# Turning the layers' input whole, and one block of programs with the weights converted between the first batch's steps

## The chip, the cores and the metric

The kernel runs on one core of one Trainium2 chip. The metric is device time of one execution in microseconds (us). A core has five engines with programs of their own: TensorE (PE, matmuls and transposes into the eight PSUM banks), VectorE (DVE), ScalarE (ACT), GpSimd (POOL), and SyncE (SP), which here only issues DMAs. They meet by semaphores: an instruction raises one when it is done, and another engine waits for a value of it. Each engine runs its instructions strictly in the order in which they are written, so a wait holds everything behind it.

## The reference

Sixteen batches of 512 rows by 128 columns. Linear attention with 16 heads of 8, then two layers of windowed softmax attention (8 heads of 64, window 64) and a gated feed-forward. All of it is between layer norms, with residual sums.

```python
def shift_token(t):                      # the upper half of the columns comes from the row before
    t1, t2 = jnp.split(t, 2, axis=-1)
    t2 = jnp.pad(t2, ((0, 0), (1, 0), (0, 0)))[:, :-1]
    return jnp.concatenate([t1, t2], axis=-1)

def _layer(x, wqkv, qs, ksc, wo, lg, lb, w1, b1, w2, b2):
    h = shift_token(x)
    q, k, v = jnp.split(h @ wqkv, 3, axis=-1)
    ...                                  # heads, l2norm, rotary_xpos, local_attention
    x = x + o @ wo
    h = shift_token(x)
    h = (h - mu) / jnp.sqrt(var + 1e-05) * lg + lb
    a, g = jnp.split(h @ w1 + b1, 2, axis=-1)
    return x + (a * jax.nn.gelu(g, approximate=False)) @ w2 + b2

x = x + _layernorm(_L0_attn_ref(_layernorm(x), Wq, Wk, Wv, Wo))
y = _layernorm(x)
for l in range(2): y = _layer(y, ...)
out = x + _layernorm(y)
```

## The kernel before

**Steps.** The work on a batch is cut into steps, each known by kind, layer l, part j (a quarter of the 512 rows) and batch n. Linear attention: load (x_in), ln_in and norm_in (to y_rows), yt (turned to y_cols), aqkv, arope, phi, at, aq, den, expand, as (scores), mask, ao, awo, then ln_attn, norm_attn, add_mid, keep (a copy of x_in goes to DRAM), ln_mid and norm_mid (to x_res0, the layers' input). Per layer: h (the input turned, shifted by a row in the upper half, and split), per quarter qkv, sq, ss, guess, norms, rope, normalize, qkt (q and k turned), s (scores), max, exps, rden, pn, pt (probabilities turned), o, wo; then sh, ln_ffn, norm_ffn, h2t, w1, gelu, gate, w2. At the end ln_out, norm_out, bring, add_out, store.

**Order.** STARTS gives each batch a start and TIMES gives each step of each engine a time in a batch. `order_of` sorts all steps of an engine by their sum; that is the engine's program, written out in full. Some four batches are in work at once. HOLD says how long a step is meant to hold its PSUM bank; `banks_of` gives out the eight banks by it, and `take` makes PE wait for the step that used the bank before (RELEASED names the signal).

**Signals.** `Signal` makes one semaphore per layer. They start at a value of four batches (`start`), so that waits on earlier steps of the first batches hold at once; 128 semaphores are raised so.

**The turn h.** On PE (lines 709 to 722) the bank's lower 64 partitions get four transposes of columns 0 to 63 (line 721). Its upper 64 get matmuls of columns 64 to 127 with the identity, one row further on (line 719), so that the shift lies in where the result is put; a one-column matmul of an identity with a column whose upper half is zero clears row 0 (line 716). ACT copies the bank to h_cols as float16 (line 911), DVE takes the rest that this leaves, bank minus copy, as a second float16 (line 1134). qkv (line 732) multiplies in three passes per 512 columns: high by high, high by low weights, then low by high weights, the first to wait for DVE.

**Linear weights and layer weights.** They live in SBUF once: w_la and wo_la_t are turned on PE, wqkv and w1 are scaled and split into two float16 halves by ACT (line 533) and DVE (line 545), the rotary tables are multiplied by the q and k scales (line 557), the masks and an identity are cast (lines 547 to 549). The kernel has two blocks. The first one loads all weights with one semaphore (38 DMAs), converts them, clears buffers and starts the signals; the second runs the steps. Between blocks all engines meet.

## Time and profile before

| | us |
|---|---|
| median of 3 runs | 1832.37 (1830.87 to 1837.60) |
| the profiled execution, its own time | 1839.22 |
| its span, first to last instruction | 1836.7 |
| granted PE clock, mean over the span | 0.971 |
| x_in loads issued at | 35.68, 87.52, 172.70, 273.74, 377.93, 481.87, ... 1523.3 |

The page gives busy time per engine, a chain of work that ended last, and groups of instructions. A timeline gives each engine's instructions in order of time, equal neighbours merged (x8 means eight of them); behind a row in brackets stands how long the engine had been idle and what released it. The loads of x_in mark the batches: their distance is the time of one batch.

### The profile page before, as it was taken

How to read it: one execution, taken by the hardware profiler on the slowest of the kernel's cores; microseconds unless marked ns; L12 is line 12 of the kernel's file. 1: busy time of each engine (PE TensorE's matmuls, PEld its weight loads, DVE VectorE, ACT ScalarE, POOL GpSimd, SP SyncE). 2: the span in 40 equal slices, each digit the busy share in tenths (PEclk: the TensorE clock that was granted, in tenths of full speed). 3: DMA queues.
4: the chain of work that ended last, by engine and by line, in shares of the span. 5: the costliest groups of instructions: out<-in, count | busy, mean ns of one | idle time of the engine just before them, and what ended most of it. 6: DMA issues, size and time to landing. Idle time of an engine off the chain costs nothing.

```text
span 1836.7 us, 51372 instructions
## 1 busy us (share of the span) xinstructions
PE 1641.0 (89%) x18212; PEld 1149.2 (63%) x18340; DVE 1329.3 (72%) x3471; ACT 1367.3 (74%) x4277; POOL 1285.8 (70%) x1715
## 2 busy tenths in 40 slices
PE   0677989999999999999999999999999999998875
PEld 0344666666667666666666666666667666666653
DVE  2465777877777787877778787777777787776552
ACT  1264768787887878798887878787787878788663
POOL 1263777777777887777777787777777887777562
PEclk9888999999999999999999999999999999999986
DMA  3000001011111011111111011111101011111001
GB/s 117 12 16 19 22 23 25 18 36 30 36 28 28 19 34 27 31 36 30 36 28 28 19 31 30 31 36 28 39 22 31 22 25 36 30 31 30 19 21 29
DMA packets 58135, 54.52 MB, mean 30 GB/s; under 512 B 7538, under 2 KB 42780, under 8 KB 57756
## 3 DMA queue, kind: packets, MB, share of 16 engines
q1 hardware_dynamic: 57884, 51.25, 11.0%
q8 instruction: 149, 2.44, 0.5%
q14 instruction: 102, 0.84, 0.2%
HBM read 13.48 MB, written 8.39 MB: 12 GB/s over the span
## 4 chain that ended last, share of the span: by engine, by line
PE 70%; ACT 12%; POOL 7%; issue 6%; DVE 3%; DMA 0%; POOLq 0%; ACTq 0%; DVEq 0%; SPq 0%
PE bank L732 10%; PE bank L787 7%; PE bank L759 7%; PE bank L798 5%; PE bank L744 5%; PE bank L771 5%; PE bank L838 4%; PE bank L827 4%; PE bank L679 4%; PE bank L695 3%; PE bank L753 2%; PE bank L719 2%; ACT probs L959 2%; ACT probs_t L853 2%; POOL qk_rows L1308 2%
## 5 line engine op out<-in xcount | busy, mean ns | idle before, releaser
L959 ACT ACTIVATE probs<-bank,s_low 128x128 f32<-128x128 f32 x1024 | 360.1, 384 | 60.7 <-DVE s_low L1171 60.6
L1308 POOL TENSOR_TENSOR qk_rows<-qk_rows,qk_tmp 128x512 f32<-128x512 f32 x256 | 328.2, 1282 | 16.6 <-DVE qk_tmp L1159 15.8
L1321 POOL TENSOR_TENSOR probs<-probs,s_rden 128x512 f32<-128x512 f32 x256 | 263.5, 1050 | 68.1 <-DVE s_rden L1180 68.1
L732 PE MATMUL bank<-wqkv_sb,h_cols 128*128 128x512 f16 x1152 | 281.2, 388 | 7.9 <-ACT probs_t L853 2.6
L1311 POOL TENSOR_TENSOR qk_rows<-qk_rows,qk_rnorm 128x512 f32<-128x512 f32 x256 | 268.7, 1050 | 20.1
L959 ACT ACTIVATION_READ_ACCUMULATOR probs<-bank,s_low 128x1 f32 x1024 | 229.0, 224 | 0.0
L1156 DVE TENSOR_TENSOR qk_rows<-bank,rope 128x512 f32<-128x512 f32 x256 | 174.4, 681 | 39.2 <-POOL qk_rows L1311 35.4
L1126 DVE TENSOR_TENSOR room<-bank,const 128x512 f32<-128x512 f32 x256 | 158.7, 683 | 57.8 <-PE bank L679 56.2
L732 PEld LDWEIGHTS bank<-wqkv_sb,h_cols 128*128 128x128 f16 x1152 | 108.2, 99 | 142.7 <-issue 22.7
L853 ACT ACTIVATE probs_t<-bank 128x512 f32<-128x512 f32 x256 | 140.9, 598 | 67.9 <-PE bank L771 65.2
L1142 DVE TENSOR_REDUCE qk_sum<-qk_sq 128x16 f32<-128x1024 f32 x128 | 155.1, 1212 | 46.2 <-ACT qk_sq L918 44.2
L1171 DVE TENSOR_REDUCE s_low<-bank 128x4 f32<-128x512 f32 x256 | 164.3, 684 | 30.6 <-PE bank L759 30.6
L1159 DVE TENSOR_TENSOR qk_tmp<-bank,rope 128x512 f32<-128x512 f32 x256 | 174.3, 681 | 0.0
L918 ACT ACTIVATE qk_sq<-bank 128x512 f32<-128x512 f32 x256 | 144.4, 618 | 22.9 <-PE bank L732 22.2
L798 PE MATMUL bank<-wo_sb,o_cols 128*128 128x128 f32 x1024 | 141.0, 281 | 19.4 <-DVE room L1126 12.5
L744 PE MATMUL bank<-const,qk_rows 128*128 128x128 f32 x1024 | 140.8, 281 | 15.4 <-POOL qk_rows L1311 12.6
L798 PEld LDWEIGHTS bank<-wo_sb,o_cols 128*128 128x128 f32 x1024 | 129.5, 195 | 38.1 <-DVE room L1126 24.9
L771 PE MATMUL bank<-const,probs 128*128 128x128 f32 x1024 | 142.5, 280 | 8.8 <-POOL probs L1321 6.8
L787 PE MATMUL bank<-probs_t,v_even 128*64 128x64 f32 x2048 | 133.2, 228 | 17.6 <-ACT probs_t L853 10.1
L759 PEld LDWEIGHTS bank<-k_cols,q_cols 64*64 64x64 f32 x4096 | 112.3, 134 | 55.5 <-issue 55.5
L759 PE MATMUL bank<-k_cols,q_cols 64*64 64x128 f32 x4096 | 143.4, 278 | 0.0
L827 PE MATMUL bank<-h_cols,w_sb 128*128 128x512 f16 (+1 forms) x576 | 139.6, 386 | 2.1 <-ACT h_cols L990 0.9
(154 smaller groups left out, 3650.6 us busy)
## 6 DMA issues: line engine op xcount, KB each, us to landing
v_even<-v_rows SPq DMA_DIRECT2D x224, 128.0 KB, 2.3
x_in<-in_L_attn_x SPq DMA_DIRECT2D x16, 256.0 KB, 3.2
kept_rows<-x_in SPq DMA_DIRECT2D x16, 256.0 KB, 2.3
x_back<-kept_rows SPq DMA_DIRECT2D x16, 256.0 KB, 3.0
out<-x_back SPq DMA_DIRECT2D x16, 256.0 KB, 2.4
room<-in_constants SPq DMA_DIRECT2D x1, 1024.0 KB
hidden<-in_L_ffn_wqkv SPq DMA_DIRECT2D x1, 768.0 KB
qk_rows<-in_L_ffn_wqkv SPq DMA_DIRECT2D x1, 768.0 KB
```

Source lines behind the costliest of these rows:

```text
L732: mm = pe.matmul(to[:, :], h_cols[st.l][:, x_half, st.j * P:(st.j + 1) * P], wqkv_sb[:, st.l, w_half, w * INNER:(w + 1) * INNER], start=(n ...
L744: mm = pe.transpose(to[:, c * P:(c + 1) * P], qk_rows[st.l][:, a, w, c * P:(c + 1) * P], ident)
L759: mm = pe.matmul(to[half][w * WIN:(w + 1) * WIN, c * P:(c + 1) * P], q_cols[st.l][rows, a, c, w * WIN:(w + 1) * WIN], k_cols[st.l][rows, c ...
L771: mm = pe.transpose(to[:, c * P:(c + 1) * P], probs[st.l][:, half * PAIRS + c, :], ident)
L787: mm = pe.matmul(to[half * DH:(half + 1) * DH, c * P + w * WIN:c * P + (w + 1) * WIN], values[l][:, a, head * DH:(head + 1) * DH], probs_t ...
L798: mm = pe.matmul(to[:, 0:D], o_cols[st.l][:, c * P:(c + 1) * P], wo_sb[:, st.l, c, :], start=(c == 0), stop=(c == PAIRS - 1))
L827: mm = pe.matmul(to[0:n, :], w1_sb[:, st.l, w_half, half * HID + at_:half * HID + at_ + n], h2_cols[:, x_half, :], start=(p == 0), stop=(p ...
L853: return act.activation(to, of, ACT.Copy)
L959: act.activation(probs[st.l][:, n, :], bank[b[half]][:, c * P:(c + 1) * P], ACT.Exp, bias=s_low[st.l][:, a, n:n + 1], accum_out=s_sum[st.l ...
L1308: pool.tensor_tensor(rows(w), rows(w), qk_tmp[l][:, w, :], ALU.add).then_inc(pool_qk.of(st), 1)
L1311: pool.tensor_tensor(heads64(rows(w)), heads64(rows(w)), qk_rnorm[l][:, a, w * HEADS:(w + 1) * HEADS].unsqueeze(2).to_broadcast([P, HEADS, ...
L1321: pool.tensor_tensor(probs[l][:, mine, :], probs[l][:, mine, :], s_rden[l][:, a, mine].unsqueeze(2).to_broadcast([P, PAIRS, P]), ALU.mult) ...
```

## The change

**The turn.** PE does four whole transposes of 128 by 128 into the bank; the matmuls of lines 716 and 719 go. The shift moves to ACT and DVE: each does its work in two instructions, one for the lower 64 partitions and 512 columns, one for the upper 64 partitions, which reads bank columns 0 to 510 and writes h_cols columns 1 to 511. Column 0 of the upper half is cleared once at the start. act_h and dve_h count two per batch, and qkv waits for both.

**One block.** The first block is gone. SP loads the first batch's x_in, the four linear weights and the constants, then the weights of layer 0, then of layer 1, each group with a semaphore of its own. Each engine starts its own signals. The weights wait in buffers of layer 1 (qk_rows1, probs1, probs_t1, qk_tmp1, o_cols1) that no batch needs yet, where before they lay in `room`. ACT splits layer 0's weights after the fourth av and layer 1's after the first ao of batch 0; DVE does its part after den 1, mask 0, mask 3 and ln_mid of batch 0. The first qkv and rope of each layer wait for it.

**The table.** STARTS, TIMES and HOLD are all new.

```diff
-STARTS = [8839, 22968, 37104, 51237, ...
+STARTS = [3891, 18013, 32146, 46280, ...
...
-        "h": [[17736], [35934]],
+        "h": [[16859], [35929]],
...
-        act_h = signal("act_h", DEPTH, 1)
+        act_h = signal("act_h", DEPTH, 1, 2)
...
-        dve_h = signal("dve_h", DEPTH, 1)
+        dve_h = signal("dve_h", DEPTH, 1, 2)
...
-        setup_const = room[:, 4 * D:4 * D + NSETUP]
+        setup_const = qk_rows[1][:, :, :, :].rearrange("p a w n -> p (a w n)")[:, 0:NSETUP]
+        la_rows = o_cols[1]
...
-        with nc.Block() as block:
-            @block.sync
-            def _(sp):
-                sp.dma_start(const[:, :], consts[:, 0:NCONST]).then_inc(loaded, 16)
...
+        def start_signals(engine, mine):
+            for sig in every:
+                if sig.name.split("_")[0] in mine:
                     for sem in sig.sems:
+                        engine.sem_inc(sem, sig.start())
...
+                start_signals(sp, ("x", "out", "v", "sh"))
+                for at, (_, st) in enumerate(order["sync"]):
+                    if at > 0:
+                        run(st)
+                        continue
+                    sp.dma_start(x_in[:, :, :], rows_of(x, st)).then_inc(x_loaded.of(st), 16)
+                    load_first()
+                    for l in range(DEPTH):
+                        load_layer(l)
+                    sp.wait_ge(zeroed, ZEROED)
...
-                    pe.matmul(to[DH:P, 0:1], ident[:, DH:P], cst("causal")[:, 0:1], start=True, stop=True)
                     for j in range(NT):
-                        n = min(P, T - 1 - j * P)
-                        pe.matmul(to[DH:P, j * P + 1:j * P + 1 + n], x_res[st.l][0:n, j, DH:D], ident[0:n, 0:n],
-                                  start=True, stop=True)
-                        mm = pe.transpose(to[0:DH, j * P:(j + 1) * P], x_res[st.l][:, j, 0:DH], ident)
+                        mm = pe.transpose(to[:, j * P:(j + 1) * P], x_res[st.l][:, j, :], ident)
                     mm.then_inc(pe_h.of(st), 1)
...
+                start_signals(pe, ("pe",))
+                pe.wait_ge(first_loaded, 16 * FIRST_LOADS)
+                for n in range(4):
+                    mm = pe.transpose(bank[0][:, n * D:(n + 1) * D], la_rows[:, n * D:(n + 1) * D], ident)
+                mm.then_inc(turned, 1)
+                pe.wait_ge(la_ready, 2)
                 for _, st in order["tensor"]:
+                    if st.kind == "qkv" and st.n == 0 and st.j == 0:
+                        pe.wait_ge(ready[st.l], READY[st.l])
...
-                    copy(h_cols[st.l][:, 0, :], bank[b[0]][:, :]).then_inc(act_h.of(st), 1)
+                    copy(to[0:DH, 0, :], bank[b[0]][0:DH, :]).then_inc(act_h.of(st), 1)
+                    copy(to[DH:P, 0, 1:T], bank[b[0]][DH:P, 0:T - 1]).then_inc(act_h.of(st), 1)
...
+                def halve(l):
+                    act.wait_ge(loaded[l], 16 * LOADS[l])
+                    for whole, halves in ((whole_wqkv[l], wqkv_sb[:, l, :, :]), (whole_w1[l], w1_sb[:, l, :, :])):
+                        act.activation(halves[:, 0, :], whole, ACT.Copy, scale=W_SCALE).then_inc(halved, 1)
...
+                    if st.name() == ("av", 0, NT - 1, 0):
+                        halve(0)
+                    if st.name() == ("ao", 0, 0, 0):
+                        halve(1)
...
-                    dve.tensor_tensor(h_cols[st.l][:, 1, :], bank[b[0]][:, :], h_cols[st.l][:, 0, :],
+                    dve.tensor_tensor(to[0:DH, 1, :], bank[b[0]][0:DH, :], to[0:DH, 0, :],
+                                      ALU.subtract).then_inc(dve_h.of(st), 1)
+                    dve.tensor_tensor(to[DH:P, 1, 1:T], bank[b[0]][DH:P, 0:T - 1], to[DH:P, 0, 1:T],
                                       ALU.subtract).then_inc(dve_h.of(st), 1)
...
+                dve.wait_ge(first_loaded, 16 * FIRST_LOADS)
+                dve.wait_ge(zeroed, ZEROED)
+                turn_linear()
                 for _, st in order["vector"]:
+                    if st.kind == "rope" and st.n == 0 and st.j == 0:
+                        dve.wait_ge(ready[st.l], READY[st.l])
                     run(st)
+                    if st.name() == ("den", 0, 1, 0):
+                        lower_weights(0)
+                    if st.name() == ("mask", 0, 0, 0):
+                        turn_tables(0)
+                        turn_masks()
+                    if st.name() == ("mask", 0, 3, 0):
+                        lower_weights(1)
+                    if st.name() == ("ln_mid", 0, 0, 0):
+                        turn_tables(1)
```

On PE, layer 0's turn in the middle of the run, before (line 798 is wo, 732 is qkv):

```order
L716 MATMUL bank1<-const 64x1 [waits act_ln_mid_0,dve_wo_1]
L719 MATMUL bank1<-const,x_res0 64x128
L721 MATMUL bank1<-const,x_res0 64x128
...
L721 MATMUL bank1<-const,x_res0 64x128
L798 MATMUL bank5<-wo_sb,o_cols1 128x128 [waits act_o_1,act_p_1]
L798 MATMUL bank5<-wo_sb,o_cols1 128x128 x3
L732 MATMUL bank3<-wqkv_sb,h_cols0 128x512 [waits act_p_1,act_h_0]
L732 MATMUL bank3<-wqkv_sb,h_cols0 128x512
L732 MATMUL bank3<-wqkv_sb,h_cols0 128x512 [waits dve_h_0]
```

and after (line 678 is the turn, 755 is wo, 689 is qkv):

```order
L678 MATMUL bank4<-const,x_res0 128x128 [waits act_ln_mid_0,act_p_1]
L678 MATMUL bank4<-const,x_res0 128x128 x3
L755 MATMUL bank0<-wo_sb,o_cols1 128x128 [waits act_o_1,dve_wo_1]
L755 MATMUL bank0<-wo_sb,o_cols1 128x128 x3
L689 MATMUL bank2<-wqkv_sb,h_cols0 128x512 [waits act_o_1,act_h_0]
L689 MATMUL bank2<-wqkv_sb,h_cols0 128x512
L689 MATMUL bank2<-wqkv_sb,h_cols0 128x512 [waits dve_h_0]
```

The turn is four instructions for nine matmul and transpose calls; behind it stand the same wo and qkv, with the same wait for dve_h at the third pass.

On ACT, from norm_mid (x_res0) to the next batch's norm_in (y_rows), before:

```order
L864 ACTIVATE x_res0<-x_in,ln_nmr_mid0,ln_rstd_mid0 128x128 [waits pool_rstd_mid_0,dve_wo_0]
L864 ACTIVATE x_res0<-x_in,ln_nmr_mid0,ln_rstd_mid0 128x128 x3
L959 ACTIVATE probs1,s_sum1<-bank7,s_low1 128x128 [waits dve_max_1,pe_pt_1]
...
L959 ACTIVATE probs1,s_sum1<-bank0,s_low1 128x128 [waits dve_max_1]
...
L853 ACTIVATE o_cols1<-bank1 128x512 [waits pe_wo_1,pe_o_1]
L853 ACTIVATE h_cols0<-bank6 128x512 [waits pe_h_0]
L938 ACTIVATE v_rows1<-bank3 128x512 [waits v_low1_1,pe_o_1,pe_qkv_1]
L990 ACTIVATE h2_cols<-bank4,ln_cols 128x512 [waits pe_w1_1,pe_h2t_0]
L990 ACTIVATE h2_rows<-bank4,ln_cols 128x512
L864 ACTIVATE y_rows<-x_in,ln_nmr_in0,ln_rstd_in0 128x128 [waits pool_rstd_in_0,pool_xmid_0]
```

and after:

```order
L829 ACTIVATE x_res0<-x_in,ln_nmr_mid0,ln_rstd_mid0 128x128 [waits pool_rstd_mid_0,dve_wo_0]
L829 ACTIVATE x_res0<-x_in,ln_nmr_mid0,ln_rstd_mid0 128x128 x3
L926 ACTIVATE probs1,s_sum1<-bank0,s_low1 128x128 [waits dve_max_1,pe_pt_1]
...
L926 ACTIVATE probs1,s_sum1<-bank6,s_low1 128x128 [waits dve_max_1]
...
L818 ACTIVATE o_cols1<-bank2 128x512 [waits pe_wo_1,pe_o_1]
L818 ACTIVATE h_cols0<-bank0 64x512 [waits pe_h_0]
L818 ACTIVATE h_cols0<-bank0 64x511
L957 ACTIVATE h2_cols<-bank5,ln_cols 128x512 [waits pe_w1_1,pe_h2t_0]
L957 ACTIVATE h2_rows<-bank5,ln_cols 128x512
L829 ACTIVATE y_rows<-x_in,ln_nmr_in0,ln_rstd_in0 128x128 [waits pool_rstd_in_0,pool_xmid_0]
...
L905 ACTIVATE v_rows1<-bank4 128x512 [waits v_low1_1,pe_o_1,pe_qkv_1]
```

h is two copies, and the copy of v (v_rows1) has moved behind y_rows.

On DVE, in the first batch behind den 1 (line 1119 before, 1097 after), before:

```order
L1119 RECIPROCAL la_rden<-la_rden 128x16 [waits dve_aden_0]
L1126 TENSOR_TENSOR room<-bank,const 128x512 [waits pe_as_0,pe_ao_0]
L1126 TENSOR_TENSOR room<-bank,const 128x512 [waits pe_as_0] x3
L1126 TENSOR_TENSOR room<-bank,const 128x512 [waits pe_as_0,pe_ao_0]
L1126 TENSOR_TENSOR room<-bank,const 128x512 [waits pe_as_0] x3
```

and after:

```order
L1097 RECIPROCAL la_rden<-la_rden 128x16 [waits dve_aden_0]
L1226 TENSOR_SCALAR b_cols<-b_cols 128x1 [waits weights_loaded_0]
...
L1230 SCALAR_TENSOR_TENSOR wqkv_sb<-hidden,wqkv_sb 128x1536 [waits weights_halved]
L1230 SCALAR_TENSOR_TENSOR w_sb<-probs,w_sb 128x682 [waits weights_halved]
L1076 SCALAR_TENSOR_TENSOR la_phi<-la_tb,la_phi 128x256 [waits act_aexp_0]
L1104 TENSOR_TENSOR room<-bank,const 128x512 [waits pe_as_0,pe_ao_0]
L1104 TENSOR_TENSOR room<-bank,const 128x512 [waits pe_as_0] x3
L1239 SCALAR_TENSOR_TENSOR rope<-qk_rows,qk_tmp 128x64 x16
L1245 CAST ident_h<-const 128x128
L1246 CAST mask_h<-qk_rows 128x512
...
L1104 TENSOR_TENSOR room<-bank,const 128x512 [waits pe_as_0,pe_ao_0]
L1104 TENSOR_TENSOR room<-bank,const 128x512 [waits pe_as_0] x3
```

The splitting of layer 0's weights (line 1230) stands ahead of the third phi and of the first mask, the tables and casts (1239 to 1247) between the first two masks.

## Rows read from the trace of the kernel before

**Rows 1.** The page, part 1: busy us, share of the span, instructions.

```profile
PE 1641.0 (89%) x18212; PEld 1149.2 (63%) x18340; DVE 1329.3 (72%) x3471; ACT 1367.3 (74%) x4277; POOL 1285.8 (70%) x1715
```

**Rows 2.** Busy time by stretches: start:end, length, engines busy (instructions), PEclk, DMA share, GB/s.

```profile
4.00:6.00 2.00, 0.00 (x0) 0.00 (x0) 0.00 (x0) 0.00 (x0) 2.00 (x2) 1.00 0.96 368
...
36.00:89.00 53.00, 27.97 (x233) 16.99 (x233) 24.08 (x84) 12.28 (x34) 13.33 (x18) 0.87 0.04 12
482.00:585.90 103.90, 99.66 (x1140) 70.59 (x1147) 82.56 (x214) 84.73 (x268) 79.98 (x106) 1.00 0.12 30
```

**Rows 3.** Waits of PE, 482 to 586 us: total, times, longest (us).

```profile
PE bank L640 <- ACT y_rows L864: 1.0, 1, 1.0
...
PE bank L787 <- ACT probs_t L853: 0.3, 1, 0.3
```

**Rows 4.** Timeline of PE around layer 0's turn: start, length (us), engine, line, operation.

```profile
466.73 1.16 PE L705 MATMUL bank<-wo_la_t,y_cols 128*128 128x128 f32 x8
...
484.00 0.28 PE L716 MATMUL bank<-const 128*64 128x1 f32 x2
...
486.40 1.06 PE L798 MATMUL bank<-wo_sb,o_cols 128*128 128x128 f32 x8
487.29 2.37 PE L732 MATMUL bank<-wqkv_sb,h_cols 128*128 128x512 f16 x9
490.69 0.63 PE L640 MATMUL bank<-const,y_rows 128*128 128x128 f32 x4 [1.02 <-ACT y_rows L864]
491.15 1.04 PE L771 MATMUL bank<-const,probs 128*128 128x128 f32 x8
```

**Rows 5.** Timeline of ACT, DVE and POOL beside it.

```profile
480.15 1.65 ACT L864 ACTIVATE x_res<-x_in,ln_nmr_mid,ln_rstd_mid 128x128 f32<-128x128 f32 x4
...
484.44 0.61 ACT L853 ACTIVATE o_cols<-bank 128x512 f32<-128x512 f32 x1
...
485.01 0.87 DVE L1027 BATCH_NORM_STATS2 ln_stats_in<-x_in 128x6 f32<-128x128 f32 x4 [2.08 <-DMA x_in<-in_L_attn_x]
...
486.48 0.19 DVE L1180 RECIPROCAL s_rden<-s_sum 128x8 f32<-128x8 f32 x1
...
486.60 0.60 ACT L853 ACTIVATE h_cols<-bank 128x512 f16<-128x512 f32 x1 [1.54 <-PE bank L721]
...
487.23 0.69 DVE L1134 TENSOR_TENSOR h_cols<-bank,h_cols 128x512 f16<-128x512 f32 x1 [0.56 <-ACT h_cols L853]
...
487.73 0.20 POOL L1250 TENSOR_TENSOR ln_nmr_in<-ln_nmr_in,ln_rstd_in 128x4 f32<-128x4 f32 x1
...
488.90 1.65 ACT L864 ACTIVATE y_rows<-x_in,ln_nmr_in,ln_rstd_in 128x128 f32<-128x128 f32 x4
```

**Rows 6.** Groups of one batch, 482 to 586 us, shapes apart: busy us, mean ns.

```profile
L1000 ACT ACTIVATE hidden<-bank,b_cols 128x512 f32<-128x512 f32 x4 | 2.5, 684 | 0.0
...
L1000 ACT ACTIVATE hidden<-bank,b_cols 85x512 f32<-85x512 f32 x2 | 1.4, 685 | 0.1
```

**Rows 7.** Timeline of the start: loads and the first statistics.

```profile
0.72 0.40 SPq L484 DMA_DIRECT2D const<-in_constants  x1
...
19.70 0.43 SPq L502 DMA_DIRECT2D room<-in_L_ffn_k_scale  x1
...
35.68 0.38 SPq L588 DMA_DIRECT2D x_in<-in_L_attn_x  x1
38.50 0.87 DVE L1027 BATCH_NORM_STATS2 ln_stats_in<-x_in 128x6 f32<-128x128 f32 x4 [3.13 <-DMA x_in<-in_L_attn_x]
```

**Rows 8.** Timeline of the start: conversions, and the first batch's masks.

```profile
22.90 1.49 ACT L533 ACTIVATE wqkv_sb<-hidden 128x1536 f16<-128x1536 f32 x1 [20.91 <-DMA room<-in_L_ffn_k_scale]
...
24.42 1.76 DVE L545 SCALAR_TENSOR_TENSOR wqkv_sb<-hidden,wqkv_sb 128x1536 f16<-128x1536 f32 x1 [1.25 <-ACT wqkv_sb L533]
...
30.31 4.39 DVE L557 SCALAR_TENSOR_TENSOR rope<-room 128x64 f32<-128x64 f32 x32
...
57.74 4.88 DVE L1126 TENSOR_TENSOR room<-bank,const 128x512 f32<-128x512 f32 x8 [2.12 <-PE bank L679]
```

More of the change, by code:

```diff
@@ L163 @@
[L163 to L170 removed]
+        "norm_in": [[3712]],
@@ L474, in build @@
[L474 removed]
+        whole_w1 = [of[:, :, :].rearrange("p h n -> p (h n)")[:, 0:2 * HID] for of in (probs[1], probs_t[1])]
+        qk_scale = qk_tmp[1][:, :, :].rearrange("p w n -> p (w n)")[:, 0:DEPTH * 2 * DH].rearrange(
             "p (l w c) -> p l w c", l=DEPTH, w=2)
[L476 removed]
+        first_loaded = ctx.enter_context(nc.semaphore("first_loaded"))
```

322 lines of the change are left out of this document (161 added, 161 removed), and 32 rows, old and new, of tables (HOLD, TIMES).

## The prediction

> **What bounds the kernel now.** Read the busy shares of the page first [rows 1]: TensorE (PE) is busy 89% of the span, the three others 70 to 74%. Then the busy time by stretches [rows 2]. The span has three parts. Up to 36 us the weights are loaded and converted and no batch runs. From 36 to 89 us the first batch goes alone through linear attention and PE works 28 of 53 us: latency sets the pace. In the middle a batch takes 104.0 us (x_in is loaded every 104 us), and of 103.9 us PE is busy 99.7; ScalarE (ACT) 84.7, VectorE (DVE) 82.6. So in the middle an instruction less on PE is worth its time, as long as PE doesn't then wait. PE waits little there; its longest named wait is 1.0 us, for y_rows of the next batch [rows 3].
>
> The profiled execution took 1839.2 us, of which 1836.7 are span; I sum against 1839.2. The median of the runs shown is 6.9 us below it, and I take 6.9 off at the end.
>
> **The layer's turn on PE.** Before, a turn (h) begins at 484.00 and the next step at 486.40: 2.40 us of PE [rows 4]. Its replacement is four whole transposes, the same four instructions as the turn of y_rows, which begins at 490.69 and gives way at 491.15: 0.46 us. That is 1.94 us less PE, twice per batch, 32 times in all.
>
> **What ACT and DVE pay.** Each copy of the turned bank becomes two, over 64 partitions and 512 or 511 columns. A copy's time doesn't go by partitions: the same gelu took 684 ns on 128 partitions and 685 on 85 [rows 6]. So each half costs a whole one: ACT +0.5 to 0.6 us per turn, DVE +0.6 to 0.7 (their rows are 0.60 and 0.69, and neighbours overlap by some 0.1) [rows 5]. Per batch ACT goes to 85.9 and DVE to 84.0 us: neither becomes the bound by its load. What counts is who waits for the two copies.
>
> **Layer 0: the gain is lost to a path.** On PE the turn is followed by one step (wo, 0.89 us) and then by the qkv matmuls, whose third pass waits for the lower half from DVE; that is so before and after. Follow the path from the end of norm_mid (x_res, 481.80) [rows 5]: it frees x_in, the next batch's rows are loaded, DVE takes its statistics at 485.01 (+3.2), is free behind a reciprocal at 486.6 (+4.8), and only then comes DVE's part of h, 487.23 to 487.92 (+6.1). PE's first qkv group runs from 487.29 and, with 2.37 us where the others take 2.10, waits 0.25 in it. After, DVE is free at +4.8 and does two halves, 1.3 us: +6.1 again. So the third pass can't come earlier than +6.2, whatever PE saves before. Nor does the part ahead shrink: from the end of awo (467.89) to the end of norm_mid are 13.9 us of DVE, POOL and ACT in a row, in the same order before and after, with the same PE steps beside them. ACT makes PE wait already at wo: it has exps (2.75 us) and the copy of o between norm_mid and the h copies, o_cols is there at +3.3, wo can begin at +3.4 instead of +2.6, qkv at +4.5. I book 0 for layer 0's turn; its bounds are -1.94 (no wait) and +0.7 (DVE is late by a whole half).
>
> One wait goes: PE's y step came at 490.69, +8.9, held by ACT, which did h, v, two h2 copies and then y_rows at 488.90. In the new order v stands behind y_rows, so y_rows can begin when POOL has the scale (487.73 + 0.20, or +6.1) and ACT is free: h at +3.3 to +4.4, h2 to +5.7, then y_rows +6.2 to +7.8. qkv's last pass leaves PE about then. PE's y step at +7.95: 0.95 us sooner. Bounds 0 and -1.0 [rows 3].
>
> **Layer 1: the gain stays.** There several steps stand between the turn and qkv, in both orders (some 12 us of PE work), so nobody waits for the longer copies: -1.94.
>
> Per batch in the middle: -1.94 - 0.95 = -2.9, a period of 101.1. Bounds -3.9 (all PE time of both turns) and 0 (the new order waits as much more elsewhere; see the rivals). Sixteen batches, less one for the ends, where PE isn't the bound: 15 x 2.9 = -43.5 (0 to -58).
>
> **The order's table.** All steps are placed anew and so are the banks, but on PE the sequence of kinds is nearly the one before. Where a step now stands closer behind what it needs (s one step behind the last qkt of a layer-1 round, o one step behind a layer-0 pt), the trace of before shows what such a distance costs: o one step behind its pt waited 0.3 us [rows 3]; other pairs moved apart. I book 0, within -15 and +30 over the run, worth -1 to +2 us a batch.
>
> **The start.** Before, DVE's first statistics are at 38.50: all loads are in by 22.9, then the weights are converted, then x_in is issued at 35.68 [rows 7, 8]. After, x_in is SP's first load, then four small weights and the constants, 866 KB in all; issues follow each other by 0.5 us (38 issues from 0.72 to 19.70), the queues move 368 GB/s [rows 2], so 2.4 us of transfer, and a load of x_in lands 2.8 us after its issue (35.68 to 38.50). SP first raises 18 of the 128 signals; all 128 took less than the 15.6 us from 20.13 to 35.68 [rows 7], so 18 take under 2.2. Landed at 6.5 to 10; PE's four transposes (0.46 at full clock, twice that at half) and two DVE copies of 384 and 128 columns (0.8, by the 0.69 of 512) make 1.3 to 2: statistics at 8.5 to 12, and at up to 13 if loads behind slow it. I take 9.5: -29.0 (-25.5 to -30).
>
> The conversions (ACT 4.5 us, DVE some 11) go between the first batch's steps [rows 8]. In the first batch's own time, as before: ACT's first pair (1.49 for 1536 columns, 0.7 for 682) delays la_phi and la_qk_cols by 1.0. DVE's first pair (1.76 for 1536 columns, 0.8 for 682) now stands ahead of the third la_phi and of mask: mask can start at 58.7 instead of 57.74, +1.0, the same delay. Half the tables (2.2 of 4.39) and three casts (0.9), 3.1 us, stand between the first two masks, which ran back to back for 4.88 us: all of it on the path. Later edits hide: DVE's second pair in the 3.1 us before ln_attn's statistics, the second half of the tables behind ln_mid while POOL and ACT work; a further 0.6 for what doesn't. Sum +4.7 (bounds +2 if the masks aren't on the path, +9 if loads come late). Loads: ACT needs layer 0's weights at about 22 us; everything was landed at 22.9 before, and layer 0's half is now issued first.
>
> Sum: 1839.2 - 29.0 + 4.7 - 43.5 = 1771.4; less 6.9: **1765**.
>
> **A rule against the change.** In the middle of the run the granted clock is 1.00 (2.4 GHz); in the first batch, where PE pauses, it is 0.87 on average [rows 2]. If the new turns ran at 1.2 GHz, each would cost 0.92 us instead of 0.46: 0.9 us per batch. The Trainium skill (TensorE: Matmul & The Clock Gate, "Part 4: PE-mode transpose") says that transposes don't count as PE being busy for the clock. By that rule, more transposes and fewer matmuls speak for a lower clock; the 1.00 of the middle stretch, where each batch turns q, k and the probabilities by transposes, speaks against it.
>
> **Rivals.**
> - B, the period stays at 104: waits grow by 2.9 us a batch in the new order. For it: PE had 4 us of slack a batch, the others wait for each other on paths like layer 0's, which already eats one turn. Then only the start gains: 1839.2 - 24.3 - 6.9 = 1808.
> - C, everything is had: 3.9 us a batch: 1765 - 15 = 1750. For it: the new order was free to put work between turn and qkv elsewhere. Against: the third pass.
> - D, slower: at layer 0 PE has only its o step and the short turn (1.5 us) while ACT does norm_mid, exps and the copy of o (1.65 + 2.75 + 0.6 = 5.0 us) before wo may start. Before, the wo of the round ahead, s and the long turn stood there too, 6 us with the o step (480.4 to 486.40). If PE comes to o just when ACT has turned the probabilities, it waits 3.5 us there, and if the same happens at s behind qkt and at the layer-1 rounds, 6 us a batch are lost: 1808 + 15 x 3.1 = 1854. It decides from 4.5 us of new waits a batch on (2.9 + 24.3 / 15).
> - E, the clock: the turns run at 1.2 GHz: 1765 + 15 x 0.9 = 1779.
> - F, the loads of the layers or the conversions hold the first batch up, +9 to +14: 1770 to 1780.
>
> **Chances.** Forecast 0.55, B 0.2, C 0.1, D 0.05, E 0.03, F 0.07. The range reaches from below C to just past B, 1745 to 1812, and leaves out D and tails. About 0.5% (9 us) is what a measurement of this kernel can tell from no change: faster than 1823 0.92, within 0.04, slower 0.04.
>
> **What would show it.** ln_stats_in first at 8.5 to 12 us; x_res of batch 0 ends near 63 (87.4 before, less 24.3); x_in loads 101 us apart; the turn 0.46 us on PE; in the first qkv group of a batch PE waits for h_cols of ACT and DVE, some 2 us in all, at layer 1 not at all; the wait for y_rows gone; clock 1.00. Wrong if the period is 103 or more, if it is near 100 with no wait at h, or if the first batch's end moved by under 18 us.

## The result, and the profile after

| | before | after |
|---|---|---|
| median of 14 runs each | 1835.1 us (1830.9 to 1837.7) | 1847.3 us (1839.0 to 1852.3) |
| ratio | 1 | 1.0063 [1.0049, 1.0078] |
| the profiled execution, its span | 1836.7 | 1839.2 |
| granted PE clock, mean | 0.971 | 0.951 |
| first statistics at | 38.50 | 10.06 |
| second load of x_in (norm_mid of batch 0 over) | 87.52 | 70.04 |
| distance of the loads in the middle | 104.0 | 105.8 |

The change made the kernel 0.6% slower; the forecast was 1765 (1745 to 1812). The profile of after gained 17.5 us by the second load and gave 21.0 back between it and the last one (1526.8, before 1523.3). It is one of the faster executions of after (1841.0 us, at a granted clock of 0.951; the median of the fourteen is 1847.3 at 0.946), so its trace shows 6 us less of the loss than the medians do.

The page of after, PE's busy time and its clock in 40 slices (9 is 90% or more):

```profile
PE 1653.1 (90%) x18020; PEld 1161.9 (63%) x18020; DVE 1373.9 (75%) x3503; ACT 1383.7 (75%) x4309; POOL 1281.4 (70%) x1717
...
PEclk8798999999999999999999999999999999999988
```

PE is busy for longer than before (1641.0 us) although it has less to do [rows 1], and the clock's digits show 9 for the whole middle, as before. The finer view shows what happens. These are the stretches of one batch, from one load of x_in to the next (columns as in [rows 2], PEclk third from the end):

```profile
468.52:472.90 4.38, 2.32 (x42) 1.84 (x41) 1.83 (x12) 4.33 (x20) 0.00 (x0) 1.00 0.28 90
472.90:476.30 3.40, 3.03 (x11) 2.26 (x12) 2.59 (x8) 3.18 (x7) 3.12 (x4) 0.53 0.00 0
476.30:517.40 41.10, 39.97 (x394) 27.45 (x392) 35.05 (x85) 36.38 (x119) 32.48 (x47) 1.00 0.13 31
517.40:520.80 3.40, 3.40 (x40) 2.61 (x37) 2.57 (x4) 1.71 (x8) 3.32 (x4) 0.51 0.00 0
```

Twice in a batch, for 3.4 us, PE runs at a granted clock near 0.5, which is 1.2 GHz; before, this stretch had 1.00 [rows 2]. The first time lies 4 to 8 us behind the load, the second 49 to 52. Not every batch looks like this one: of ten, six have both stretches, one has the second alone, and in three (from 786.0, 892.2 and 997.9) the first is 6.8 us long and the second is missing. PE's named waits in the batch shown:

```profile
PE bank L755 <- DVE x_att L1166: 2.4, 1, 2.4
PE bank L640 <- DVE room L1104: 0.5, 1, 0.5
```

The wait for y_rows [rows 3] is gone, as forecast; a wait of 2.4 us for x_att at wo, line 755, has come in its place. PE around layer 0's turn (compare [rows 4]):

```profile
470.19 0.66 PE L678 MATMUL bank<-const,x_res 128*128 128x128 f32 x4
473.27 2.08 PE L755 MATMUL bank<-wo_sb,o_cols 128*128 128x128 f32 x8 [2.43 <-DVE x_att L1166]
475.14 2.80 PE L689 MATMUL bank<-wqkv_sb,h_cols 128*128 128x512 f16 x9
477.77 0.60 PE L601 MATMUL bank<-const,y_rows 128*128 128x128 f32 x4
```

The turn (470.19) ends after 0.66 us and then PE stands still for 2.4. The step it waits with is wo of layer 1, round 1 (wo11). Its bank was last used by wo10, the wo of the round ahead, and DVE gives that back late:

```profile
471.47 0.87 DVE L1005 BATCH_NORM_STATS2 ln_stats_in<-x_in 128x6 f32<-128x128 f32 x4 [2.47 <-DMA x_in<-in_L_attn_x]
...
472.94 0.28 DVE L1166 TENSOR_TENSOR x_att<-x_res,bank 128x128 f32<-128x128 f32 x1
...
473.25 0.63 DVE L1113 TENSOR_TENSOR h_cols<-bank,h_cols 64x512 f16<-64x512 f32 x1
473.91 0.69 DVE L1115 TENSOR_TENSOR h_cols<-bank,h_cols 64x511 f16<-64x511 f32 x1
```

In the new order DVE adds wo10 (x_att, 472.94) behind the statistics of the next batch, which wait for the load that norm_mid frees; before, it stood ahead of them (482.64, statistics at 485.01 [rows 5]):

```profile
482.64 0.29 DVE L1185 TENSOR_TENSOR x_att<-x_res,bank 128x128 f32<-128x128 f32 x1 [1.72 <-PE bank L798]
```

The other place is the first linear-attention score step, as of round 0 (as00). It has four row groups, and the table gives each of them a bank:

```profile
510.15 0.66 PE L678 MATMUL bank<-const,x_res 128*128 128x128 f32 x4
510.64 0.59 PE L710 MATMUL bank<-mask_h,ident_h 128*128 128x512 bf16 x2
...
514.78 1.52 PE L640 MATMUL bank<-room,la_qk_cols 32*128 32x512 f32 x4
516.75 1.39 PE L640 MATMUL bank<-room,la_qk_cols 32*128 32x512 f32 x4 [0.45 <-DVE room L1104]
```

The third group takes the bank of the first and waits for DVE to mask it. With the old order the four have four banks and run beside each other in 1.14 us (here in e4, which keeps the old order):

```profile
508.03 1.14 PE L640 MATMUL bank<-room,la_qk_cols 32*128 32x512 f32 x8 [0.26 <-DVE h_cols L1115]
```

The start (compare [rows 7] and [rows 8]), first statistics and first mask:

```profile
10.06 0.86 DVE L1005 BATCH_NORM_STATS2 ln_stats_in<-x_in 128x6 f32<-128x128 f32 x4
```

```profile
36.87 2.48 DVE L1104 TENSOR_TENSOR room<-bank,const 128x512 f32<-128x512 f32 x4 [2.90 <-PE bank L640]
```

### The profile page after: what moved, and what is told of

The parts are those of the page before. It is cut to its first block, busy times and chain, and to the rows that moved or that the text cites. A ratio compares the mean times of both kernels' runs of the same rounds, so it can differ in the third digit from the quotient of the medians.

```text
span 1839.2 us, 50920 instructions
## 1 busy us (share of the span) xinstructions
PE 1653.1 (90%) x18020; PEld 1161.9 (63%) x18020; DVE 1373.9 (75%) x3503; ACT 1383.7 (75%) x4309; POOL 1281.4 (70%) x1717
## 3 DMA queue, kind: packets, MB, share of 16 engines
q1 hardware_dynamic: 57884, 51.25, 10.8%
## 4 chain that ended last, share of the span: by engine, by line
PE 64%; ACT 15%; POOL 7%; issue 6%; DVE 5%; DMA 3%; SPq 0%; POOLq 0%; ACTq 0%; DVEq 0%
PE bank L689 12%; PE bank L640 5%; PE bank L716 5%; PE bank L744 5%; PE bank L701 5%; PE bank L755 5%; ACT probs L926 5%; PE bank L795 5%; PE bank L728 4%; PE bank L784 4%; PE bank L656 3%; DMA x_in<-in_L_attn_x 3%; PE bank L710 2%; POOL probs L1349 2%; ACT probs_t L818 2%
## 5 line engine op out<-in xcount | busy, mean ns | idle before, releaser
L689 PE MATMUL bank<-wqkv_sb,h_cols 128*128 128x512 f16 x1152 | 289.7, 399 | 10.2 <-DVE h_cols L1115 5.8
L755 PE MATMUL bank<-wo_sb,o_cols 128*128 128x128 f32 x1024 | 152.0, 295 | 45.9 <-DVE x_att L1166 34.6
L755 PEld LDWEIGHTS bank<-wo_sb,o_cols 128*128 128x128 f32 x1024 | 137.3, 206 | 60.6 <-DVE x_att L1166 37.7
L744 PE MATMUL bank<-probs_t,v_even 128*64 128x64 f32 x2048 | 139.7, 235 | 10.2 <-ACT probs_t L818 5.1
L701 PE MATMUL bank<-const,qk_rows 128*128 128x128 f32 x1024 | 136.0, 278 | 9.4 <-POOL qk_rows L1339 9.1
L744 PEld LDWEIGHTS bank<-probs_t,v_even 128*64 128x64 f32 x2048 | 110.7, 144 | 48.7 <-issue 17.8
```

The source lines that it names most:

```text
L689: mm = pe.matmul(to[:, :], h_cols[st.l][:, x_half, st.j * P:(st.j + 1) * P], wqkv_sb[:, st.l, w_half, w * INNER:(w + 1) * INNER], start=(n ...
L701: mm = pe.transpose(to[:, c * P:(c + 1) * P], qk_rows[st.l][:, a, w, c * P:(c + 1) * P], ident)
L744: mm = pe.matmul(to[half * DH:(half + 1) * DH, c * P + w * WIN:c * P + (w + 1) * WIN], values[l][:, a, head * DH:(head + 1) * DH], probs_t ...
L755: mm = pe.matmul(to[:, 0:D], o_cols[st.l][:, c * P:(c + 1) * P], wo_sb[:, st.l, c, :], start=(c == 0), stop=(c == PAIRS - 1))
```

## The experiments

"Old order" is the table of times and banks of before, "new order" that of after. Every kernel was timed beside before on the same chip; before's own median on these chips lay between 1834.9 and 1836.8 us, so medians of different rows compare to some 2 us. "Undisturbed" periods are the distances of x_in loads in the middle of the profiled execution in which the clock stayed at 1.00; the last two columns count, of ten or eleven such distances, those with PE near half clock at the first place (from 4 to 7 us behind the load on) and at the second (from 48 to 51 on).

| kernel | median, us | ratio to before | undisturbed period | 1st | 2nd |
|---|---|---|---|---|---|
| before | 1835 | 1 | 103.9 to 104.4 | 0 | 0 |
| e1 turn alone | 1819.1 | 0.991 [0.990, 0.993] | 102.3 to 103.4 | 1 | 0 |
| e2 new order alone | 1859.2 | 1.014 [1.011, 1.017] | 104.6 to 105.0 | 1 | 2 |
| e3 start alone | 1818.2 | 0.991 [0.989, 0.993] | 103.6 to 104.9 | 0 | 0 |
| e4 start and turn, old order | 1798.2 | 0.980 [0.978, 0.983] | 102.3 to 103.4 | 0 | 0 |
| e5 start and new order, old turn | 1841.2 | 1.003 [1.002, 1.004] | 105.0, 105.2 | 6 | 2 |
| after | 1847.3 | 1.006 [1.005, 1.008] | none | 9 | 7 |

**The three parts, one at a time.** e1 takes before and changes the turn only, e2 the two tables only, e3 the start only, e4 is after with the old tables, e5 after with the old turn.

> The kernel before with only the turn changed: four whole transposes on PE, each copy on ACT and DVE in two halves; old order and banks, old start. Theory O (the new order and banks cost the time, the turn helps): period 101 to 102 us instead of 104, total 1835 less 30 to 45 = 1790 to 1805, granted clock of the middle 1.00. Theory T (the turn itself costs: later copies, or a lower clock because PE pauses behind a shorter turn): period 105 to 106, total 1850 to 1865, granted clock about 0.97 as in the changed kernel.

> The kernel before with only the table of the order and the banks of after; old turn, old start. Theory O: the table costs about 5 us a batch more than the turn gives back: period 107 to 109, total 1880 to 1915, PE waits of 2 us or more at wo for DVE's x_att in each batch and two stretches at half clock. Theory T: period 103 to 104, total 1820 to 1835, clock 1.00.

> The kernel before with only the start changed: x_in loaded first, one block, conversions between the steps of the first batch; old order, banks and turn. Both theories: the middle stays at 104 us a batch and 1.00 of clock, and the total falls by what the start gains: 28.4 at the first statistics less what the conversions cost the first batch. If that is the 4.7 of the forecast, 1835 - 24 = 1811; if it is the 10.9 that the changed kernel shows and the order has no part in it, 1835 - 17.5 = 1817.

> The changed kernel with the order and banks of before: new start, new turn. Theory O: both gains, period 101 to 102, total 1770 to 1790, well below both kernels. Theory T: only the start is had and the turn costs 1.9 us a batch: 1817 + 30 = 1847, as the changed kernel.

> The changed kernel with the old turn (nine matmuls and transposes, one copy each on ACT and DVE): new start, new order and banks. If the new order costs the same beside either turn, the period is the 105.0 of the table alone, the granted clock of the middle 1.00, and the total 1859 less 17 = 1842. If the two stretches at half clock come from the order and not from the turn, the clock is 0.97 here too and the total 1855 or more.

The start is worth 17 us, the turn 16, both together 37 (e4, 2% below before and the fastest design found); the 4 us by which the two together exceed their sum are not explained. The turn gives some 1.4 us a batch in either order where the clock is undisturbed (104.0 to 102.7; in the new order 105.0 to the 103.5 of e6 and e11 below). The new order costs 24 us alone and 49 beside the new start and turn. So theory O holds in its sign but not in its numbers: e1, expected at 1790 to 1805, took 1819, e4 (1770 to 1790) took 1798, because the turn gives less than booked, and e2 (1880 to 1915) took 1859. The order's size comes from two things: about 0.9 us a batch that it costs even at full clock, and the slow stretches, which with the old turn come in some batches and with the new turn in nearly all.

The 0.9 us can be placed. In a batch of e11 (below) at full clock, from 894.0 to 997.3, PE's score steps of linear attention (line 640) are busy 7.3 us, in a batch of e4 (459.5 to 562.1) 5.1. All of PE is busy 98.2 us there and 96.5 in e4, and idle 5.2 and 6.1. So most of it is as00, whose groups run in two pairs, one after the other.

The old turn does not keep the clock up for certain: e5 has eight slow stretches in ten batches. Nor does the length of PE's pause decide alone. In e5 the pauses at wo11 are 0.7 to 1.4 us long and six batches have the first slow stretch; e2, with the same order and turn, has pauses of 0.6 to 1.3 us and one such batch. What the different start changes there is not shown.

**What one slow stretch costs.** Theory P says that PE's pause brings the clock down. e6 gives wo11 another bank:

```diff
-    "wo": [[[2316], [1293], [2972], [2707]], [[1061], ...
+    "wo": [[[2316], [1293], [2972], [2707]], [[1110], ...
```

> The changed kernel with one number of HOLD changed (wo of layer 1, round 0: 1061 to 1110). By it the second wo of layer 1 (wo11) takes the bank that o11 used instead of the one that wo10 used and that DVE gives back only behind the next batch's statistics; the first qkv of layer 0 takes the other in turn, nothing else moves. Theory P (the pause of PE is what the bank costs, and the half clock behind it follows from the pause): the wait of 2.4 to 2.7 us at wo goes, 1 to 1.6 us of it come back at the third pass of qkv, the first of the two slow stretches goes, the second stays; period 103 to 104, clock 0.98 to 0.99, total 1847 less 25 to 40 = 1807 to 1822. Theory Q (the clock falls because the turn is transposes only, whatever PE waits for): both slow stretches stay, period 104.5 to 105, total 1832 to 1840.

1833.8 us, 0.999 [0.997, 1.001], 12 us above the range of P. The wait of 2.4 is split, in the first batch shown below, into 1.0 for o_cols, 1.2 for x_att at the first qkv (which now has wo10's bank: I had written so, without asking who gives it back) and 0.7 for h_cols. The slow stretch at the first place is left in 3 of 10 batches, at the second in 5. Three batches in a row:

```profile
573.82:678.32 104.50, 99.20 (x1120) 70.29 (x1127) 84.82 (x217) 85.49 (x270) 79.95 (x106) 0.98 0.12 30
678.32:783.38 105.06, 99.75 (x1121) 71.24 (x1128) 85.37 (x217) 85.47 (x270) 79.82 (x106) 0.98 0.12 29
783.38:886.71 103.33, 98.21 (x1121) 69.90 (x1128) 84.84 (x217) 85.35 (x270) 79.97 (x106) 1.00 0.12 30
```

The two with one slow stretch take 104.5 and 105.1 us, the one without 103.3. One costs 1.2 to 1.8 us here; in e5 and e2 a batch with one takes 105.7 to 106.5 and 106.0 to 106.6, one without some 105.0, so about 1 there. After's 105.8 is 103.5 plus two of 1.2.

**The order of DVE, not the bank.** e11 puts DVE's wo10 ahead of the statistics again (its time in the table 45983, now 45880).

> The changed kernel with one time of DVE's table changed (wo of layer 1, round 0: 45983 to 45880), by which DVE adds wo10 ahead of the statistics of the next batch's rows, as in the kernel before, and not behind them. Theory P: the bank is back before wo11 asks for it, the wait of 2.4 to 2.7 us goes, of which 1 to 1.6 us come back as waits for ACT's o_cols and DVE's lower half of h (as in the run with the old order); the first slow stretch goes in most batches, the second stays: period 103.9 to 104.6, total 1815 to 1828. If the bank is not what wo11 waits for, nothing changes: 1847.

1831.1 us, 0.997 [0.996, 0.999], 3 us above P's range. As P said the wait for x_att is gone; 1.0 for o_cols and 1.0 to 1.6 for h_cols take its place. Slow stretches: 1 and 4. But the undisturbed period is 103.4 to 103.7, as in e6, where part of that wait was left. The wait itself cost next to nothing: the third pass of qkv waits for DVE's lower half anyway. What it cost was the clock.

**Is it the pause?** The first try filled PE's pause with 14 matmuls (e9) or 21 transposes (e10) into a bank that I took to be free:

```diff
+                    if st.l == 1 and st.j == 1:
+                        pe.wait_ge(*act_v.at(Step("v", 1, 3, st.n)))
+                        spare = bank[banks_by_name["qkv", 1, 3, st.n][2]]
+                        for _ in range(14):
+                            pe.matmul(spare[:, P:4 * P], ident_h[:, :], mask_h[:, 0, 0:3 * P], ...)
```

> The changed kernel, with 14 matmuls (bf16, 384 columns, 0.16 us each at full clock, 2.3 us in all) on PE ahead of wo11, into a bank that nobody else uses there; their result is not read. They stand in the place of the pause behind the layer-0 turn. Theory P (the pause makes the clock fall): the slow stretch 4 to 9 us behind norm_mid is gone in nearly all batches, the other at 48 to 53 stays; wo11 begins when it began before, and the period falls by what one slow stretch costs, from 105.8 to about 104.7: total 1847 less 17 = 1830. Theory R (the fall comes from something else at that place, or the power of more work): the stretch stays, total 1847 or more.

> The same place and length, filled with 21 transposes of 128x128 (0.11 us each at full clock) instead of matmuls. If PE being busy is all that counts for the clock, this is as the run with matmuls: first slow stretch gone, 1830. If transposes do not count as work for the clock, as the Trainium skill says (TensorE: Matmul & The Clock Gate, Part 4: PE-mode transpose), the slow stretch stays or comes sooner, and the total is 1847 to 1860.

1927.4 and 1931.2 us, 1.049 [1.047, 1.052] and 1.050 [1.046, 1.054]: the bank was not free.

```profile
PE bank L756 <- ACT v_rows L911: 6.3, 1, 6.3
```

ACT copies v of round 3 only behind this place, so the filler waited 6.3 us first. As a test of the filler they failed. They show the other end: with the longer pause (5.9 to 6.9 us in e9) the slow stretch comes in every one of ten batches and lasts 7 to 10 us. e13 and e14 wait for o_cols, as wo11 does anyway, and fill the rest, 1.4 us, in the bank that o11 left; with 9 matmuls or 12 transposes.

> The changed kernel with the pause behind the layer-0 turn filled in a better place: PE waits for o_cols first (1.0 us behind the turn, as before), then does 9 matmuls (bf16, 384 columns, 1.4 us at full clock) into the bank that o11 has just left, then waits for the bank of wo10 as before. wo11 begins when it began before. Theory P (the pause makes the clock fall): the slow stretch 4 to 9 us behind norm_mid is gone in most batches, the other one stays, the period falls from 105.8 to about 104.7, total 1847 less 17 = 1830 (1825 to 1838). Theory R (not the pause): the slow stretch stays in 9 of 10 batches, total 1843 to 1852.

> The same with 12 transposes of 128x128 (1.4 us at full clock) in place of the 9 matmuls. If the engine's being busy is all that counts, as the run with matmuls: 1830. If transposes do not count as work for the clock (the Trainium skill, TensorE: Matmul & The Clock Gate, Part 4: PE-mode transpose), the slow stretch stays in most batches: 1843 to 1852.

```profile
580.59 1.64 PE L756 MATMUL bank<-mask_h,ident_h 128*128 128x384 bf16 x9 [0.96 <-ACT o_cols L823]
582.50 1.16 PE L760 MATMUL bank<-wo_sb,o_cols 128*128 128x128 f32 x8 [0.27 <-DVE x_att L1171]
```

1833.8 us, 0.999 [0.998, 1.001], and 1835.3, 1.000 [0.998, 1.001]. wo11 (582.50) starts 5.2 us behind norm_mid, no sooner than in after (4.8). Yet the first slow stretch is gone in 9 of 10 batches in both, and the second is still there (5 and 7). The same two places of a batch of e13:

```profile
581.40:585.00 3.60, 3.33 (x21) 1.88 (x19) 3.46 (x14) 2.95 (x7) 2.59 (x4) 1.00 0.01 2
...
625.40:629.20 3.80, 3.80 (x43) 3.13 (x40) 3.09 (x6) 2.22 (x9) 3.72 (x5) 0.55 0.00 0
```

The fill does PE's needed work no sooner and saves 12 to 14 us all the same, and over all ten runs of each the granted clock is 0.961 in the median, where after's is 0.946: theory P is shown for the first place. The first slow stretch follows from the pause, though by e2 and e5 not from its length alone. Transposes did as well as matmuls. The Trainium skill (TensorE: Matmul & The Clock Gate, "Part 4: PE-mode transpose") says that transposes don't count as PE being busy in the same way. These runs show no such difference (the first slow stretch in 1 of 10 batches with either fill), though they don't rule it out for a PE that does nothing else.

**A pause elsewhere.** e12 is e4 with DVE's lower half of h ahead of the statistics (ln_in 3336, now 3920).

> New start, new turn, old order (the best so far), with DVE's lower halves of layer 0's turn placed ahead of the next batch's statistics instead of behind them (ln_in 3336 to 3920). The path of the forecast (the third pass of qkv waits for DVE, which waits for the load that norm_mid frees): the wait for h_cols falls from 1.6 to at most 0.7 us, and the wait for y_rows comes back as 0.5 to 1.5 us, since the statistics start 1.2 us later; the two nearly cancel, period 102.2 to 103.2, total 1790 to 1806. If the lower halves are late for another reason, the wait for h_cols stays at 1.6.

1851.4 us, 1.008 [1.006, 1.011]: 53 us slower than e4. The wait for h_cols fell by half, as the path says, but y_rows came 3.1 us late, twice the most that I allowed:

```profile
PE bank L601 <- ACT y_rows L829: 3.1, 1, 3.1
...
PE bank L689 <- DVE h_cols L1115: 0.8, 1, 0.8
```

In 10 of 11 batches PE is near half clock around that wait, somewhere from 9 to 17 us behind the load, where e4 never is.

**The second place.** Three kernels move banks around as00. e7 raises its four HOLD numbers to 1500, e8 does that and e6's change, e17 exchanges only the bank of its third group with the one that s02 left; e18 is e17 with e11's and e16's cures.

> The changed kernel with four numbers of HOLD changed (as of round 0: 1183 to 1367 become 1500). By it the four groups of the first linear-attention score step (as00) take four different banks; in the changed kernel its third group takes the bank of its first and waits until DVE has masked it. Theory P: that step takes 1.1 to 1.5 us instead of 3.1 with its wait, the second slow stretch goes, the first stays; period 105.85 less 2 to 3.5 = 102.5 to 104, total 1795 to 1817. Theory Q: the step gains at most 1.5 and both slow stretches stay: period 104.3 or more, total 1825 or more.

> The changed kernel with both changes of HOLD. Theory P: clock 1.00 throughout, both gains, period 100.5 to 102.7, total 1760 to 1798, at or below the 1798 of new start and new turn with the old order. Theory Q: clock still below 0.99, period 103.5 or more, total 1812 or more.

> The changed kernel; from as00's third group on, the bank of its first group and the bank that s02 left are exchanged, in all that follows, so no other step comes closer to the user before it than 6 steps. Theory P: as00 takes about 2.0 us in place of 3.2 with its pause of 0.46, the second slow stretch (48 to 53 us) is gone in most batches, the first stays: period 105.8 less 1.2 (clock) and up to 1.2 (the step) = 103.5 to 104.7, total 1847 less 18 to 36 = 1811 to 1829. Theory M (the mask on DVE sets the pace there, not PE): the clock stays at 1.00 there but the period falls by the clock's 1.2 at most: 1829. Theory N (the banks are not what makes PE slow there): unchanged, 1847.

> The same, with DVE adding wo10 ahead of the next batch's statistics, and the first conversion waiting for POOL's la_phi. Theory P: nearly no slow stretches, period 102.3 to 103.5, total 1785 to 1803, as fast as the old order with the new turn (1798) or faster. If slow stretches come back elsewhere (a pause moved, not removed): 1810 to 1830.

e7 took 1914.2 us (1.043 [1.041, 1.045]), e8 1931.2 (1.053 [1.050, 1.055]), e17 1857.8 (1.012 [1.011, 1.014]), e18 1835.4 (1.000 [0.999, 1.001]). None did what I expected. In e7 the next o step got the bank of the turn h10, which DVE's lower half still reads:

```profile
PE bank L755 <- DVE x_att L1166: 2.9, 1, 2.9
PE bank L744 <- DVE h_cols L1115: 2.1, 1, 2.1
```

It waits 2.1 us for it, and PE is slow there for 7 to 10 us. In e17 the bank that s02 left is still read by ACT's exps:

```profile
631.24 1.51 PE L646 MATMUL bank<-room,la_qk_cols 32*128 32x512 f32 x4
633.52 1.13 PE L646 MATMUL bank<-room,la_qk_cols 32*128 32x512 f32 x4 [0.77 <-ACT probs L932]
```

The second slow stretch is there in 8 of 10 batches of e17. So neither way tried to give as00 four banks left every step near it with a free one: the new order puts as00, which takes four, directly behind pt01, where before two steps stood between. e18 has slow stretches at the second place in 6 of 10 batches. That PE's pause and its slow, one-after-another groups there bring the clock down is likely by the first place, but it isn't shown, since no run took them away in the new order; the old order has neither.

**Which layer's turn.** e15 is e4 with the old turn in layer 0.

> New start, old order, new turn in layer 1 only; layer 0 turns as before, with one copy each on ACT and DVE. By the terms of the forecast layer 0's turn is worth nothing and layer 1's all: the period is that of both turns (102.7) or shorter, without the wait of 1.6 us for h_cols, total 1798 or less. If layer 1's gain is what is lost (ACT and DVE later by one copy, waits of 0.7 for v_rows and 0.3 for a bank behind it), the period is 103.3 to 104.0 and the total 1806 to 1818.

1807.4 us, 0.985 [0.983, 0.986], undisturbed 103.3 to 103.8. Layer 1's turn is worth 10.8 us (from e3's 1818.2), layer 0's 9.2 (to e4). In the middle a batch takes 104.1 us in e3, 103.4 in e15 and 102.7 in e4 (means of eleven): each turn is worth 0.7. Why layer 1 gives a third of its 1.94 is seen beside each other, e3 (old turn) and e4 (new). PE's turn, ACT's h_cols and v_rows, then PE's pt (line 732 or 728):

```profile
604.53 0.28 PE L677 MATMUL bank<-const 128*64 128x1 f32 x2
...
607.12 0.60 ACT L822 ACTIVATE h_cols<-bank 128x512 f16<-128x512 f32 x1 [1.08 <-PE bank L682]
...
608.26 0.60 ACT L907 ACTIVATE v_rows<-bank 128x512 f32<-128x512 f32 x1
...
609.82 1.09 PE L732 MATMUL bank<-const,probs 128*128 128x128 f32 x8
```

```profile
602.66 0.60 PE L678 MATMUL bank<-const,x_res 128*128 128x128 f32 x4
...
604.08 1.23 ACT L818 ACTIVATE h_cols<-bank 64x512 f16<-64x512 f32 x2
...
606.08 0.60 ACT L905 ACTIVATE v_rows<-bank 128x512 f32<-128x512 f32 x1
...
606.73 1.15 PE L728 MATMUL bank<-const,probs 128*128 128x128 f32 x8 [0.66 <-ACT v_rows L905]
```

With the old turn ACT waits 1.08 us for PE. With the new one the bank is there at 603.3, but ACT has exps until 604.1, then copies twice, 1.23 us in place of 0.60. v_rows starts 3.4 us behind the turn's start instead of 3.7, PE waits 0.66 for it, and pt starts at +4.1 instead of +5.3: 1.2 of the 1.94 are left here, and as00 waits 0.26 for the bank of h a little later (508.03, shown above); what takes the rest was not traced.

**The first batch.** e16 is e4, with DVE's first conversion behind POOL's la_phi:

```diff
                     if st.name() == ("den", 0, 1, 0):
+                        dve.wait_ge(*pool_aq.at(Step("aq", 0, 1, 0)))
                         lower_weights(0)
```

> New start, new turn, old order, and DVE's first conversion of weights waits until POOL has scaled la_phi of round 1, so that the two no longer run beside each other (0.5 us later for the conversion). Theory S (a large two-input operation on DVE holds POOL up): POOL's operation takes 0.41 to 0.46 us in place of 2.76, the mask of round 1 begins 2.3 us sooner (34.7 to 32.4), and the first batch ends 1.5 to 2.3 sooner; total 1796 less 2. Theory V (POOL's operation is long for another reason, such as the DMA traffic of the loads): it takes 2.7 us again and the total is 0.5 later.

After, the conversion (DVE, two inputs in SBUF) and POOL's la_phi beside each other; the second row is POOL's:

```profile
31.11 1.74 DVE L1230 SCALAR_TENSOR_TENSOR wqkv_sb<-hidden,wqkv_sb 128x1536 f16<-128x1536 f32 x1
31.13 3.10 POOL L1313 TENSOR_TENSOR la_phi<-la_phi,la_rden 128x128 f32<-128x128 f32 x1 [1.26 <-DVE la_rden L1097]
...
34.29 0.47 PE L631 MATMUL bank<-const,la_phi 128*128 128x128 f32 x1 [4.46 <-POOL la_phi L1313]
```

e16:

```profile
28.97 0.41 POOL L1314 TENSOR_TENSOR la_phi<-la_phi,la_rden 128x128 f32<-128x128 f32 x1
...
30.55 2.47 POOL L1305 TENSOR_TENSOR room<-la_qk_cols,const 128x512 f32<-128x512 f32 x1 [1.18 <-ACT la_qk_cols L818]
...
32.05 2.47 DVE L1104 TENSOR_TENSOR room<-bank,const 128x512 f32<-128x512 f32 x4
```

POOL's operation takes 0.41 us in place of 2.76 (3.10 in after), and it is now the next one (room, 2.47 instead of 1.04) that meets the conversion. The mask begins at 32.05 instead of 34.70, the second load at 67.3 instead of 69.9: theory S. The total, 1799.1 (0.980 [0.978, 0.981]), shows nothing of 2 us. The Trainium skill (SBUF — State Buffer, "Who interferes with whom") says that a DVE instruction with two SBUF inputs and a POOL instruction that reads SBUF shut each other out for the whole instruction; the rows agree: in after and in e16 the long POOL operation ends only behind DVE's second conversion (34.23 behind 33.63, 33.02 behind 32.13).

## Why the prediction was wrong, step by step

Two of its own signs of being wrong came out: the period is 105.8 us, over 103, and the first batch's end moved by 17.5 us, under 18. The 6.9 us that it took off for the median came from three runs; from fourteen they are 4.1, which would have made it 1767.

**The start** was right: first statistics forecast at 9.5, measured 10.06; -28.4 for -29.0.

**The conversions in the first batch** were mis-sized: +4.7 booked, +11.0 in after (from first statistics to second load 49.0 before, 60.0 after). The tables and casts between the masks cost the 3.1 booked. What stands ahead of the first mask was booked at 1.0 and cost 7.6 (mask at +19.2 before, at +26.8 after). 2.6 of it is POOL shut out by DVE (34.70 in e4, 32.05 in e16), for which the sum had no term. Some 2 to 3.5 are the new order: the first mask comes at +24.8 in e4 and +26.8 in after, and in e2, which has the new order and no conversions there, at +22.7 (60.95 less 38.24) where before has +19.2. The rest is not separated.

**Layer 0's path** came out in its numbers, and in part by luck. In e4 norm_mid ends at 459.44; the third pass begins at 465.46, +6.0 (forecast not before +6.2), and the y step at 467.41, +8.0 (forecast +7.95):

```profile
461.57 0.66 PE L678 MATMUL bank<-const,x_res 128*128 128x128 f32 x4
...
462.84 1.13 PE L755 MATMUL bank<-wo_sb,o_cols 128*128 128x128 f32 x8 [0.61 <-ACT o_cols L818]
...
463.81 0.60 ACT L905 ACTIVATE v_rows<-bank 128x512 f32<-128x512 f32 x1
...
464.71 0.69 DVE L1115 TENSOR_TENSOR h_cols<-bank,h_cols 64x511 f16<-64x511 f32 x1
...
465.46 1.68 PE L689 MATMUL bank<-wqkv_sb,h_cols 128*128 128x512 f16 x7 [1.02 <-DVE h_cols L1115]
...
465.62 1.64 ACT L829 ACTIVATE y_rows<-x_in,ln_nmr_in,ln_rstd_in 128x128 f32<-128x128 f32 x4
...
467.41 0.63 PE L601 MATMUL bank<-const,y_rows 128*128 128x128 f32 x4 [0.27 <-ACT y_rows L829]
```

PE waits 0.6 and 1.0 there at wo and qkv (forecast: some 2 us, at qkv alone). The third pass waits for DVE as the forecast said. The y step has another reason than the one given: the forecast moved v behind y_rows, but e4 has the old order with v ahead of it (463.81), and y_rows begins at +6.2 all the same, since ACT no longer waits 1.54 us for PE's turn [rows 5]. In the new order, without the bank's wait (e11), the two come at +6.6 and +8.4. The layer-0 term, -0.95, measured -0.7.

**Layer 1, "nobody waits for the longer copies"**, was wrong: -1.94 booked, -0.7 measured. The steps between the turn and qkv are PE's; ACT was busy when the bank came, and pt waited for what ACT does behind the copy.

**"The table of order", booked at 0** within -1 to +2 us a batch, is the term that failed: +3.1 us a batch, 49 us over the run. I compared the order of kinds on PE. What counted was which bank a step gets and who gives it back: wo11 on wo10's bank with DVE's add moved behind a load, and as00 on its own. Both stood in the order of after, which could be read before any run: the wo behind the turn there waits for dve_wo_1 and before did not.

**The clock**: rival E priced the turns at 1.2 GHz, 0.9 us a batch. The turns (470.19 and 510.15) run ahead of the slow stretches, at full clock; it is 3.4 us of what comes behind the pause, or 6.8, that run at half. No term had a price for that, so a wait of 2.4 us that the path hides was not free after all.

**Rival D** had the right place (PE waits at the wo behind layer 0's short turn) and the right sign, but named ACT; it was DVE and a bank. It said that 4.5 us of new waits a batch decide. 2.4 and 0.5 did, with the clock, and with a start that gained less than D had set against them.

In sum, from the runs: 104.0 - 1.4 (turn) + 0.9 (order) + 2.3 (two slow stretches) = 105.8 us a batch. The 2.3 is what is left of the 105.8, and agrees with two stretches of 1.2.

## What to carry to other kernels

When work on the bounding engine gets shorter, look at what the others do at the moment when the result is ready: the gain is cut there. A new order or bank table is a change of its own; go through each step near the edit and ask which bank it takes, who gives that back, and what stands before the giver on its engine. And try such a table apart from the edit: the edits here were worth 2%, and the table that came with them took all of it. Mending one place can move the wait: e6, e7 and e17 gave a step of the new order another bank, and PE waited for that bank or at a step close by.
